# A fused decoder layer on one core: adapters loaded ahead of the output weights, attention operands in four transfers

## The reference: what is computed

```python
x = x + attn(layernorm(x))       # 32 query heads, 8 key/value heads, head size 32, no mask; binary weights:
                                 #   s = mean(|w|, axis=1); y = x @ sign(w / s).T * (s * scale)   for q, k, v, o
x = x + xattn(layernorm(x))      # read / 16-head causal attention with rope / write / gated MLP / write, on 4 streams of 256
x = x + ffn(layernorm(x))        # 1024x1024 kernel + low-rank adapters: lora_A, lora_B gated per batch row, and shared ones
```

## Time and profile before

| | us |
|---|---|
| median of 3 runs | 1079.12 (1075.88 to 1081.67) |
| profiled execution, its own time | 1087.15 |
| its span, first to last instruction | 1085.4 |
| busy PE / DVE / ACT / POOL | 913.9 / 678.3 / 416.2 / 320.3 |
| mean granted TensorE clock | 0.878 |

### The profile page before, as it was taken

How to read it: one execution, slowest core, us unless ns; L and a number is a source line. 1 busy time by engine, 2 the same in 40 slices (tenths; PEclk the granted TensorE clock), 3 DMA queues, 4 the chain that set the end, 5 groups by cost and what they waited for, 6 DMA issues and landing times.

```text
span 1085.4 us, 16475 instructions
## 1 busy us (share of the span) xinstructions
PE 913.9 (84%) x5546; PEld 530.1 (49%) x5546; DVE 678.3 (62%) x1397; ACT 416.2 (38%) x796; POOL 320.3 (30%) x301
## 2 busy tenths in 40 slices
PE   4896699898989899977878679994769999999996
PEld 2552354354545454444545444442655666566643
DVE  7833367676767676547676665623357876696762
ACT  4555115565646565602222225552222233233310
POOL 2200003455656565713100013442022222231210
PEclk8999799999989998988999755665769999999997
DMA  8387533324342423110223845311000110110011
GB/s 315 111 291 250 132 143 125 88 80 110 86 102 68 120 79 102 36 68 15 83 73 102 262 120 126 74 43 41 11 1 1 39 36 4 39 39 11 20 30 49
DMA packets 75557, 95.60 MB, mean 88 GB/s; under 512 B 24225, under 2 KB 47825, under 8 KB 74866
## 3 DMA queue, kind: packets, MB, share of 16 engines
q1 hardware_dynamic: 73506, 84.08, 26.7%
q10 hardware_dynamic: 2000, 10.87, 2.8%
HBM read 65.09 MB, written 29.43 MB: 87 GB/s over the span
## 4 chain that ended last, share of the span: by engine, by line
PE 57%; DVE 15%; DMA 8%; ACT 7%; SPq 5%; issue 5%; POOL 2%; DVEq 0%; ACTq 0%; POOLq 0%; PEldq 0%
PE psum L1975 6%; PE psum L1643 5%; PE psum L1912 5%; PE psum L1556 4%; DMA q_op<-q_scr 4%; PE psum L1676 4%; PE psum L1755 3%; PE psum L1688 3%; PE psum L1699 3%; PE psum L1897 3%; PE psum L1857 3%; PE psum L1748 2%; DMA region_w<-in_w_o 2%; PE psum L1960 2%; PE psum L1846 2%
## 5 line engine op out<-in xcount | busy, mean ns | idle before, releaser
L1207 DVE TENSOR_REDUCE m_neg<-psum 128x1 f32<-128x512 f32 x256 | 165.7, 682 | 78.5 <-PE psum L1643 78.5
L875 ACT ACTIVATE region_x<-psum 128x512 f32<-128x512 f32 x256 | 143.0, 598 | 109.6 <-PE psum L1676 107.5
L665 POOL TENSOR_TENSOR region_p<-region_x 128x2048 f32<-128x2048 f32 x32 | 146.7, 4583 | 86.7 <-PE psum L1699 48.3
L1643 PE MATMUL psum<-kr,q_op 96*128 96x512 f32 x176 | 83.4, 486 | 17.9 <-DMA q_op<-q_scr 17.0
L1556 PE MATMUL psum<-region_x,region_w 128*128 128x512 f16 x320 | 74.7, 389 | 4.8 <-ACT region_w L810 4.8
L1676 PE MATMUL psum<-q_op,kr 98*128 98x512 f32 x176 | 73.2, 423 | 0.4 <-ACT region_x L875 0.2
L1688 PE MATMUL psum<-region_x,v_g 128*32 128x512 f32 x512 | 70.4, 626 | 0.0
L1975 PE MATMUL psum<-ynT,region_w 128*128 128x128 f32 x512 | 64.1, 290 | 6.3 <-ACT ynT L1032 6.3
L1643 PEld LDWEIGHTS psum<-kr,q_op 96*128 96x128 f32 x176 | 34.8, 198 | 70.3 <-DVE m_neg L1207 36.5
L1975 PEld LDWEIGHTS psum<-ynT,region_w 128*128 128x128 f32 x512 | 62.6, 205 | 10.0 <-ACT ynT L1032 10.0
L1912 PE MATMUL psum<-region_a,c_o 128*128 128x512 f16 x256 | 64.0, 408 | 0.0
(11 more groups left out here) (227 smaller groups left out, 1695.5 us busy)
## 6 DMA issues: line engine op xcount, KB each, us to landing
q_op<-q_scr SPq DMA_DIRECT2D x33, 256.0 KB, 4.2
region_a<-in_x SPq DMA_DIRECT2D x8, 512.0 KB, 9.0
region_a<-in_w_q SPq DMA_DIRECT2D x8, 512.0 KB, 7.2
region_w<-in_w_o SPq DMA_DIRECT2D x8, 512.0 KB, 4.7
region_w<-in_kern SPq DMA_DIRECT2D x16, 256.0 KB, 2.8
q_scr<-region_a SPq DMA_DIRECT2D x16, 256.0 KB
kern_scr<-region_w SPq DMA_DIRECT2D x32, 128.0 KB, 1.8
region_p<-in_x SPq DMA_DIRECT2D x8, 512.0 KB, 3.3
```

What stands on the lines that cost most here:

```text
L665: pool.tensor_tensor(pair_sum[:, n], prob_a[:, 2 * n], prob_a[:, 2 * n + 1], ALU.add).then_inc(pair_ready, 1)
L875: act.activation(prob_a[:, kt, j, :], psum[:, (0, 4, 5)[(16 * k + n) % 3], :], ACT.Exp, scale=A_SCALE).then_inc(p_ready, 1)
L1207: dve.tensor_reduce(m_neg[:, k % 3, n:n + 1], psum[:, 1 + (16 * k + n) % 3, :], AX_X, ALU.max, negate=True).then_inc(s_max, 1)
L1643: pe.matmul(psum[:, 1 + (16 * k + n) % 3, :], qa_op[u][0:A_MAX, j, qt * P:(qt + 1) * P], k_op[u][0:A_MAX, :], start=True, stop=True).then_ ...
```

## The change

1. **Order.** The loads of w_o leave their place ahead of the last key stores. They are now issued behind the stores of queries 2 to 9, each after `store_q`, the first one after the query means are done; `sign_out(c)` and `abs_out(c)` move from query c to query c + 4. The o scales and the row constants (880 KB) are loaded behind the early queries. The means over w_o (`out_mean`) and the o scale (`scale_out`) move from behind the adapter products into the first attention step.
2. **Operands.** `q_scr` gets another layout, [step, head in group, part, 32, 512], and `load_qk` issues four transfers in place of six, of the same 960 KB: queries' first two parts, keys' first two parts (one source read twice), queries' third, keys' third.
3. **No clearing** of the two query operands by GpSimd; the counts of `made` go down by two.
4. **Small moves.** ACT takes the signs of the first half of w_kv between the second and the third turned tile; `turn_x(7)` goes ahead of `project_v(1)`, and `sign_q(0)` behind `turned_hi(7)`.

```diff
-        mean_w = v_g[:].rearrange("p b t e -> p (b t e)")[:, 0:P]
+        mean_w = v_g[:].rearrange("p b t e -> p (b t e)")[:, 2 * P:]
...
-        q_scr = scratch("q_scr", [2, A_KV, B, A_REP * A_HD, S])
+        q_scr = scratch("q_scr", [NI, A_REP, 2, A_HD, S])
...
-                    sp.dma_start(q_rows[part, i], stage_q(i)[part].bitcast(F32)).then_inc(staged_out[i % 4], 16)
+                    sp.dma_start(q_scr[i, :, part], stage_q(i)[part].bitcast(F32)).then_inc(staged_out[i % 4], 16)
...
-                for part in range(3):
-                    sp.dma_start(k_op[u][part * A_HD:(part + 1) * A_HD, :].bitcast(F32),
-                                 k_rows[part % 2, ds(i, 1)].rearrange("o n s -> (o n) s")).then_inc(qk_loaded[u], 16)
-                    sp.dma_start(qa_op[u][part * A_HD:(part + 1) * A_HD].bitcast(F32),
-                                 q_rows[part // 2, ds(i, 1)].rearrange("o (j e) s -> (o e) j s", j=A_REP)).then_inc(qk_loaded[u], 16)
+                sp.dma_start(qa_op[u][0:2 * A_HD].bitcast(F32),
+                             q_scr[ds(i, 1)].rearrange("o j a e s -> (o a e) j s")).then_inc(qk_loaded[u], 16)
+                sp.dma_start(k_op[u][0:2 * A_HD, :].bitcast(F32), k_rows[0, ds(i, 1)].broadcast_to([2, A_HD, S])).then_inc(qk_loaded[u], 16)
+                sp.dma_start(qa_op[u][2 * A_HD:A_MAX].bitcast(F32),
+                             q_scr[ds(i, 1), :, 0].rearrange("o j e s -> (o e) j s")).then_inc(qk_loaded[u], 16)
+                sp.dma_start(k_op[u][2 * A_HD:A_MAX, :].bitcast(F32), k_rows[1, ds(i, 1)].rearrange("o n s -> (o n) s")).then_inc(qk_loaded[u], 16)
...
-            load_o(0)
-            load_o(1)
...
-            sp.dma_start(c_o[:], d["scale_o"]).then_inc(lora_loaded, 16)
-            sp.dma_start(rows[:], d["rows"]).then_inc(w2_loaded, 16)
...
-                if i + 2 < KC:
-                    load_o(i + 2)
+                if i == 2:
+                    sp.wait_ge(means_done, 2)
+                if i >= 2:
+                    load_o(i - 2)
+            sp.dma_start(c_o[:], d["scale_o"]).then_inc(w2_loaded, 16)
+            sp.dma_start(rows[:], d["rows"]).then_inc(w2_loaded, 16)
...
-            sp.wait_ge(abs_summed, 14 + KC - 1)
             load_kern(0)
             for i in range(Q_EARLY, NI):
                 store_q(i)
+                if i < Q_EARLY + 2:
+                    load_o(i - 2)
...
-            for u in range(2):
-                pool.memset(q_op[u][:].bitcast(F32), 0.0).then_inc(made, 1)
...
+                if done == 1:
+                    pool.wait_ge(means_done, 4)
...
-            for i in range(4):
-                turned_hi(i)
+            turned_hi(0)
+            turned_hi(1)
             act.wait_ge(w_loaded[0], 32)
...
+            sign_kv(0)
+            turned_hi(2)
+            turned_hi(3)
+            sign_kv(1)
...
             for i in range(Q_EARLY):
                 q_hi(i)
-                sign_out(i)
+                if i >= 4:
+                    sign_out(i - 4)
...
             for i in range(Q_EARLY, NI):
                 q_hi(i)
+                if i < KC + 4:
+                    sign_out(i - 4)
...
             for i in range(Q_EARLY):
                 q_lo(i)
-                if i:
-                    abs_out(i)
+                if i > 4:
+                    abs_out(i - 4)
...
-            dve.wait_ge(means_done, 3)
-            for h in range(2):
-                dve.scalar_tensor_tensor(c_o[:, h * 512:(h + 1) * 512], psum[:, 5 + h, :], 1e-8, c_o[:, h * 512:(h + 1) * 512],
+            def scale_out(h):
+                dve.wait_ge(means_done, 3 + h)
+                dve.wait_ge(w2_loaded, 32)
+                dve.scalar_tensor_tensor(c_o[:, h * 512:(h + 1) * 512], psum[:, 7, :], 1e-8, c_o[:, h * 512:(h + 1) * 512],
...
                 q_lo(i)
...
+                if i < KC + 4:
+                    abs_out(i - 4)
...
+                    if done == 0 and n in (6, 13):
+                        scale_out(n // 13)
...
-            pe.wait_ge(abs_summed, 14 + KC - 1)
-            for h in range(2):
-                mm = pe.matmul(psum[:, 5 + h, :], mean_w, abs_o[:, h * 512:(h + 1) * 512], start=True, stop=True)
-            mm.then_inc(means_done, 1)
...
+            def out_mean(h):
+                if h == 0:
+                    pe.wait_ge(qk_lo, NI + 4)
+                    pe.wait_ge(abs_summed, 14 + KC - 1)
+                else:
+                    pe.wait_ge(c_ready, 4 + 4 + R4 + 1)
+                pe.matmul(psum[:, 7, :], mean_w, abs_o[:, h * 512:(h + 1) * 512], start=True, stop=True).then_inc(means_done, 1)
...
+                    if done == 0 and n in (3, 10):
+                        out_mean(n // 10)
```

61 lines of the change are left out of this document (28 added, 33 removed).

## The result

The changed kernel takes 1163.92 us (median of 4 runs, 1156.02 to 1165.9) against 1080.03 us of the kernel before (4 runs beside it, 1075.88 to 1081.67): a ratio of 1.0769, 95% interval 1.071 to 1.0828, slower. The forecast was 1150 us in a range of 1102 to 1185. A ratio is taken from those runs of a kernel that lie within about 1.5% of its fastest, so where a kernel's runs lie far apart its median and its ratio can differ. The profiled execution took 1164.25 us, of which the span is 1162.1; against the 1085.4 of the earlier trace rows the span grew by 76.7 us.

What follows compares the result with a forecast made beforehand. TensorE was taken as the bound, idle behind the early queries and at each step's operand loads. Stores 26 + cold engine 1.5 - start 2 + loads 45 = +70.5; from the median 1079.1, 1150 us, range 1102 to 1185.

Steps and rivals of the forecast that it cites:

- Rival A: Only the query stores are narrow; the keys' broadcast load spreads over sixteen engines; +4.5, 1084 us; chance 0.10.
- B: Change does what it says: new stores spread like wide ones, operand loads get faster; -31, 1048 us; chance 0.10.
- C: Transfers narrow, but each on another four engines, so no backlog; only the broadcast hurts; +35, 1114 us; chance 0.08.
- D: Forecast's mechanism, but keys at 25 GB/s and clocks that hold; +36, 1115 us; low end of the forecast's own range.
- term +26: Ahead of the steps: narrow query stores back up on four engines, moving SP's maxima transfer from 184.55 to 210.9 us.
- -2 for the start: At the start: half of ScalarE's signs moves into its idle gap, bringing the key scales 2 us earlier.
- 1.5 for a cold engine: First attention step: TensorE, warm before, comes cold out of a long hole, costing 1.5 us.
- First hole: TensorE's idle time between early queries and adapter products: products at about 129 us in place of 117.23, +12.
- Late phase: Late query stores and what queues with them on four engines: from 159 us, ending at 210.9.
- term +45: Operand loads in the steps: keys' broadcast on two engines; 34 us for thirteen loads plus 11 for the clock.
- The clock's part: In the steps: longer holes make seven steps that ran at clock 1.00 fall, 1.5 us each, 11 us.
- The signs that were named: DMA share 0.25 to 0.4 from 76 us, products 127 to 131, copy wait ending near 210, holes 3 to 5.

Runs made afterwards that it cites:

- experiment 3: Changed kernel with the old scratch and 128x512 query stores, queries in three 32-row loads, keys' broadcast load kept: 1115.03 us, ratio 1.0346.
- experiment 5: Kernel before with only the new scratch layout and narrow 4x32x512 query stores, six operand loads kept: 1120.75 us, ratio 1.0346.
- experiment 4: Changed kernel with scratch and four merged loads laid out so every new transfer's outer size is 32, 64 or 128: 1079.4 us, ratio 1.0009.
- experiment 6: Kernel before with only the small moves (signs, eighth turn of x, first query signs): 1077.02 us, ratio 0.9972.
- Experiment 10: Changed kernel with the adapters' stores put behind the last query store: 1156.38 us, ratio 1.0734.
- experiment 1: Changed kernel with its order kept, but the old scratch, 128-row query stores and six operand loads: 1069.84 us, ratio 0.9949.
- experiment 2: Changed kernel with the keys' broadcast load split into two 32-row loads, five transfers a step: 1123.49 us, runs far apart, no ratio.
- experiment 11: Experiment 7's kernel with operands in two 96-row loads instead of six of 32, high parts stored twice: 1061.97 us, ratio 0.9841.
- experiment 7: Experiment 1's kernel with the context's load moved behind the step's six operand loads: 1059.83 us, ratio 0.9814.
- experiment 9: Experiment 7's kernel with the next kernel tile's load also moved behind the operand loads: 1094.21 us, ratio 1.015.

## Why the prediction was right, and where its sum was off

**The mechanism held.** That a transfer goes to as many engines as its outer size was read from one shape in the trace of before, 4x32x512. The changed kernel shows it for the stores (0.28 and 110 GB/s from 88 to 92 us), and experiments 3 and 5 that they cost by themselves; the tail of 0.13 shows two engines for the broadcast, which was only inferred. The Trainium skill ("DMA: Bandwidth & Descriptors", "Rules for kernel authors") says that a leading zero-stride dimension of c copies confines the DMA to at most c engines; the trace agrees for two, and experiment 4, where the same zero stride lies inside, has no such tail: its load ends within a microsecond of the last full window. Rival A falls with experiment 3 (the broadcast costs 40 us), B and C with experiment 5 (the stores cost 40 us, as a backlog), and D, whose clocks hold, with the 21.1 us that the clock cost.

**Stores and order, term +26, with -2 for the start and 1.5 for a cold engine: 25.5 forecast, 32.1 measured.** The two halves of it were off in opposite directions. First hole: the products were put at 129, +12, and the start's 2 us come off that; they came at 122.93, +5.7. The remaining 4.1 us are the start again, which became 6.1 us earlier and not 2: experiment 6 gives 3.1 to the small moves and leaves 3.0 to the rest of the order. Late phase: the forecast put 51.9 us from the first late store to the last one's end (159 to 210.9); it was 60.8 (155.88 to 216.66). The term that was mis-sized is the adapters': I priced their sixteen stores by bytes, 2.6 us, and the two to b_scr at another 2.6. Experiment 10 measures 10.7 us for sixteen of the eighteen where they stand among the queries'. With all of them behind the queries' the phase is 54.3 us, 2.4 over the forecast, so 6.5 of the 8.9 us that were missed come with the place of these stores. Why they cost more than their bytes in a full queue stays open. The 1.5 us for a TensorE that comes cold out of a hole can't be told apart in any run; its busy time in the first step of the loop is 17.70 us for 16.75 before.

**What the order hides.** Experiment 1 shows a gain that I had lumped in: with wide stores the order alone brings the first operand load forward by 9.9 us (187.55 to 177.61). So the narrow stores really cost 40 to 42 us, and the order gave back 10. The forecast had priced only the two together.

**Loads, term +45 (15 to 65): +50.2 measured** over the twelve steps of the loop. The waits were forecast at 3.7 us and are 3.55 to 4.52. Their part was put at 34 us for thirteen loads, 2.6 each; measured are 28.9 for twelve, 2.4 each. The open bound was the pace of the two engines, 14 or 25 GB/s. The tail shows 23 while only keys move; an estimate with the keys' 66 KB at 23 and the other 53 KB at 14 gives 6.7 us of transport, 2.3 more than the 4.4 of before. The clock's part was too small by half: 11 us forecast, 21.1 measured. I let the seven steps that ran at 1.00 fall by 1.5 us each, as those with 2.5 us of wait do; they lost 3.1 each (109.9 us of busy time in sum became 131.5), with the clock at or under 0.85 in six of the seven. The five that had fallen before changed by 0.5 in sum. Why these dips go deeper than in the kernel before stays open. Experiments 3 and 2 give the broadcast 22.5 and 23.8 us of the waits, and experiment 3 gives it 40.5 of the whole. The 11.4 us between experiment 3 and the changed kernel (3.7 in waits) go with the narrow scratch and the 64-row queries' load, for which I had expected a gain of up to 0.4 us a load. In experiment 4, where nothing is narrow, merging still adds some 2 us of waits; the rest is the clock. The Trainium skill ("SBUF — State Buffer", "Door 1: The DMA port swizzle") says that partitions 0 to 63 reach no more ports than 0 to 31; experiment 4 agrees in that 64 rows at once gain nothing. The 96 rows of experiment 11 do gain. No run separates ports from issue times.

**Sum against own execution and median.** The sum of +70.5 was added to 1087.15 and then lowered by the 8 us by which that execution stood above the median. The profiled execution after, 1164.25, is at its median of 1163.92. The growth is 77.1 between the profiled executions and 83.9 between the medians, so 6.8 us of the miss come from that, 6.6 from the sum. In the sum itself one thing is luck: the stores' 6.6 and the loads' 5.2 too few are partly covered by the 5.6 us less behind the loop, in code that the change does not touch.

**The signs that were named.** Right: waits of 3 to 5 us behind keys, sixteen engines never full between 76 and 130 us (at most 0.82 in windows of 4 us), GpSimd's copy released late (near 210 forecast, 216.66), ScalarE waiting most for the o weights ahead of the adapter products (21.8 us from 62 to 130). Half right: the share from 76 to 130 us is 0.46 at 164 GB/s, since the o weights fill the other engines in between; only stretches with stores alone show 0.28. Wrong: products at 127 to 131 (122.93), and a clock of 0.9 or less in all steps (three have 0.92).

## What to carry to other kernels

Read a transfer's cost off its slowest dimension before its bytes: here an outer size of 4 on the stores cost 40 us and one of 2 on a broadcast another 40. The same transfers written with 32, 64 or 128 rows outside (experiment 4) took nearly all of that back, and 96 rows (experiment 11) shortened the waits. Fewer issues are worth little where the DMA engines are full between the first issue and the last landing; look at windows of 1 or 2 us there before merging. What stands on the queue ahead of an awaited load can matter as much: moving a load that nobody awaited behind it gave 10 us (experiment 1 to 7), moving one that somebody did await lost 34 (experiment 7 to 9). And count a longer wait twice: here the loop lost 28.9 us in waits and another 21.1 in the same products at a lower clock, and where experiment 7 took 2.1 us of wait out of a step, the clock gave back 1.54.

## What was not expected of the hardware

SyncE's issues slow down when the queue is full: a pair of stores that takes 0.81 us to issue in the kernel before (at 93.31) took 4.63 us in the changed one (175.44), and a single one 4.21 (at 76.46). So a backlog on four engines holds up everything behind it on SyncE, that for the twelve idle ones as well. The time of an issue did not go by size: 0.68 to 0.73 us for 64x4x512 and 0.36 to 0.42 for 32x4x512 in the changed kernel's loop, but 0.34 to 0.35 for most of 96x4x512 (experiment 11). What sets it was not tried.
